# Self attention of a Perceiver-like block: the mix of values of each tile in two halves, with the output product of the tile before it between them

## The chip, the core and the metric

The kernel runs on one core of one Trainium2 chip. The metric is device time in microseconds (us) of one execution, lower is better. A core has a matrix engine (TensorE, PE in the profile; its weight loads are listed apart as PEld), a vector engine (VectorE, DVE), a scalar engine (ScalarE, ACT), GpSimd (POOL) and SyncE (SP), which here only issues DMAs. The engines run their own instruction streams and meet at semaphores.

## What is computed

The reference is a stack of six residual blocks over x of 64 batches, 32 tokens, 256 features:

```python
x = x + _L0_xattn_ref(ctx_1024, _layernorm(x), ...)
x = x + _L0_attn_ref(_layernorm(x), ...)      # stage "sa0" of the kernel
x = x + _L0_ffn_ref(_layernorm(x), ...)       # mixture of 64 experts
x = x + _L1_xattn_ref(_layernorm(x), ctx_1024, ...)
x = x + _L1_attn_ref(_layernorm(x), ...)      # stage "sa1"
x = x + _L1_ffn_ref(_layernorm(x), ...)
```

The change touches the two self attentions. The first, shortened:

```python
q = rms_norm(proj(Wq), qn_w)          # 16 heads of 16 features
k = rms_norm(proj(Wk), kn_w)
v = proj(Wv)
scores = jnp.einsum('bhnd,bhmd->bhnm', q, k) * scale
attn = jax.nn.softmax(scores, axis=-1)
out = jnp.einsum('bhnm,bhmd->bhnd', attn, v)
return out.transpose(0, 2, 1, 3).reshape(B, N, D) @ Wo.T
```

The second (sa1) has latent queries and keys of 32 features for each head, a rotary turn, a causal mask and biases, and is otherwise alike.

## The kernel before

Both attentions are one function, `self_attention`, called once as stage sa0 and once as stage sa1. It works on NT = 16 tiles of 128 tokens (4 batches of 32 tokens each). It is a software pipeline written by hand: every engine runs the same loop over steps n from -6 to 16, and in step n it works on different tiles at different distances: a stage of the work that is called with n + 4 is four tiles ahead of the tile whose output is being finished. The order of the calls in `step` of each engine is the order of its instructions; nothing is scheduled by a planner.

In step n TensorE does, in this order: the scores of tile n + 1 (`scores`, 64 matmuls of 32x32, each of them two instructions in the trace since the data is float32); the transposes of the queries and keys of tile n + 2 (`queries_keys_T`, 8); the transpose of the normalised rows of tile n + 5 (`rows_T`, 2); the output product of tile n - 1 (`output`, 2 matmuls of 128x256, 4 in the trace); the mix of the values of tile n by its probabilities (`mix`, 64 matmuls of 32x32, 128 in the trace, after which ScalarE copies the result to yT); in sa1 one product for the latent queries (`latent_T`); and the projections of tile n + 4 (`values`, `project`). `mix` writes columns 128 to 191 of the PSUM banks 4 to 7, and `scores` writes columns 0 to 127 of the same banks. That is why `mix(n)` waits for `s.shift` of tile n + 1: VectorE has to be done with reading the scores of tile n + 1 before TensorE writes to these banks.

VectorE does in step n: `shifted(n + 1)`, which is a maximum over the scores (L2163) and their subtraction (L2167) and ends with `s.shift`; `add(n - 1)`, which waits for `s.o_ps` of the output product and adds it to the residual (L2186), with the statistics of the next norm behind it; `softmax(n + 1)` (L2172 to L2180), which ends with pT, the transposed probabilities that `mix(n + 1)` reads; then rows (L163), `queries_keys` (L2158 or L2150) and `key_sums` or `cosines` (L2132 or L2142) of tiles further ahead.

ScalarE takes the exponential (L2331) once shifted is done, and copies PSUM to SBUF (mix_T at L2337 writes yT).

Of the kernel before, what the change touches and what calls it, by code (L numbers as in the profile page):

```python
# [25 lines left out]
B, S, D = 64, 32, 256  # L26
NT = B * S // P
BT = P // S
FC = D // P
# [2036 lines left out]
def self_attention(kit, stage, weights, norm, ahead, extra, after):  # L2066


    nc = kit.nc
# [4 lines left out]
    VB = 5  # L2074
# [3 lines left out]
    with kit.stage() as st:  # L2078
        m = kit.buffers(
            st, xl=([P, 2, D], F32), xlT=([P, 2, FC, P], F32), qk=([P, 2, 2 * H, S], F32), v=([P, VB, H, S], F32), qT=([P, 2, HC, P], F32), kT=([P, 2, HC, P], F32),  # L2080
            score=([P, H, S], F32), top=([P, H], F32), prob=([P, H, S], F32), mass=([P, H], F32), rmass=([P, H], F32), pT=([P, 2, H, S], F32), yT=([P, FC, P], F32))
# [4 lines left out]
        else:  # L2086
            r = kit.buffers(st, raw=([P, 2, 512], F32), sq=([P, 512], F32), ss=([P, 2 * H], F32), rss=([P, 2, 2 * H], F32), gain=([P, 1], F32))
            w = wm.w
        s = kit.sems(stage, "zero one masked gain qb xl xlT_ps xlT qk_ps v_ps sq raw v ss scaled rss lat cosed turned qk qT_ps kT_ps qrT qrT_ps qT kT s_ps "
                     "top shift p mass rmass prob pT y_ps yT o_ps biased x_add passed")  # L2090
# [6 lines left out]
        mixed = kit.all[:, 4:8, P:P + FC * S].rearrange("p b (f q) -> p b f q", f=FC)  # L2097

        def place(h):

            return h % BT * HC + h // BT

        def past(engine, sem, value):

            if value > 0:
                engine.wait_ge(sem, value)
# [6 lines left out]
        with nc.Block(no_gpsimd_drain=True) as block:  # L2113
# [249 lines left out]
            def _(pe):  # L2363
                def rows_T(n):
                    pe.wait_ge(s.xl, n + 1)
                    past(pe, s.xlT, n)
                    for f in range(FC):
                        mm = nc.tensor.transpose(kit.psum(0)[:, f * P:(f + 1) * P], m.xl[:, n % 2, f * P:(f + 1) * P], kit.ident[:])
                    mm.then_inc(s.xlT_ps, 1)
# [8 lines left out]
                def values(n):  # L2378
                    pe.wait_ge(s.xlT, n + 1)

                    past(pe, s.x_add, n - 4)
                    past(pe, s.v, n * 2)
                    product(kit.psum(1)[:, D:2 * D], n, slice(QK, QK + D), rotary).then_inc(s.v_ps, 1)

                def project(n):
                    pe.wait_ge(s.xlT, n + 1)

                    past(pe, s.qT, n - 1)
                    past(pe, s.kT, n - 1)
                    if rotary:  # L2390
                        past(pe, s.lat, n * 2)
                        past(pe, s.cosed, n * 2)
                    else:
                        past(pe, s.raw, n)
                    for i in range(QK // 512):
                        product(kit.psum(2 + i), n, slice(i * 512, (i + 1) * 512), rotary).then_inc(s.qk_ps, 1)

                def queries_keys_T(n, more):
                    pe.wait_ge(s.qk, n + 1)

                    if more:
                        if rotary:
                            pe.wait_ge(s.lat, n * 2 + 4)
                            pe.wait_ge(s.cosed, n * 2 + 4)
                        else:
                            pe.wait_ge(s.raw, n + 2)
                    for i, done in enumerate((s.qT_ps, s.kT_ps)):
                        for c in range(HC):
                            mm = nc.tensor.transpose(kit.psum(2 + i)[:, c * P:(c + 1) * P], m.qk[:, n % 2, (i * HC + c) * BT:(i * HC + c + 1) * BT, :].rearrange("p h l -> p (h l)"), kit.ident[:])
                        mm.then_inc(done, 1)  # L2410

                def latent_T(n):
                    pe.wait_ge(s.qrT, n + 1)
                    nc.tensor.matmul(kit.psum(2), wm.wqk[:], r.qrT[:], start=True, stop=True).then_inc(s.qrT_ps, 1)

                def scores(n):
                    if n == 0 and extra is not None:

                        pe.wait_ge(extra.w, 1)
                    pe.wait_ge(s.qT, n + 1)  # L2420
                    pe.wait_ge(s.kT, n + 1)

                    past(pe, s.yT, n - 1)
                    if rotary:
                        if n == 0:
                            pe.wait_ge(s.masked, 1)
                        for a in range(BT):
                            nc.tensor.matmul(kit.all[:, 4 + a, 0:P], kit.ident16[:], r.causal[:].rearrange("p c k -> p (c k)"), start=True, stop=False, skip_group_check=True)
                    for c in range(HC):
                        for b in range(BT):  # L2430
                            for a in range(BT):
                                rows, tokens = slice(a * S, (a + 1) * S), slice(b * S, (b + 1) * S)
                                mm = nc.tensor.matmul(score[tokens, a, c, :], m.qT[rows, n % 2, c, tokens], m.kT[rows, n % 2, c, tokens],
                                                      start=not rotary, stop=True, skip_group_check=True)
                    mm.then_inc(s.s_ps, 1)

                def mix(n, more):
                    pe.wait_ge(s.pT, n + 1)

                    if more:  # L2440
                        pe.wait_ge(s.shift, n + 2)
                    for f in range(FC):
                        for i in range(2):
                            for a in range(BT):
                                for b in range(BT):
                                    rows, part, h = slice(b * S, (b + 1) * S), slice(a * S, (a + 1) * S), f * 2 * BT + 2 * a + i
                                    mm = nc.tensor.matmul(mixed[part, b, f, :], m.v[rows, n % VB, h, :], m.pT[rows, n % 2, place(h), :],
                                                          start=(i == 0), stop=(i == 1), skip_group_check=True)
                    mm.then_inc(s.y_ps, 1)

                def output(n):
                    pe.wait_ge(s.yT, n + 1)

                    pe.wait_ge(s.v, min(n + 5, NT) * 2)
                    past(pe, s.x_add, n)
                    for f in range(FC):
                        mm = nc.tensor.matmul(kit.psum(1)[:, 0:D], m.yT[:, f, :], wm.wo[:, f, :], start=(f == 0), stop=(f == FC - 1))
                    mm.then_inc(s.o_ps, 1)

                def step(n, has):  # L2460
                    if has(1):
                        scores(n + 1)
                    if has(2):
                        queries_keys_T(n + 2, has(3))
                    if has(5):
                        rows_T(n + 5)
                    if has(-1):
                        output(n - 1)
                    if has(0):
                        mix(n, has(1))  # L2470
                    if rotary and has(2):
                        latent_T(n + 2)
                    if has(4):
                        values(n + 4)
                        project(n + 4)

                    if extra is not None and n == -4:
                        extra.first_product(pe)
                    if extra is not None and n == -3:
                        extra.second_product(pe)  # L2480

                if rotary:
                    pe.wait_ge(s.one, 1)
                pe.wait_ge(weights.loaded, weights.count)
                steps(step)


# [787 lines left out]
```

## Time and profile before

| what | value |
|---|---|
| time before, median of 3 runs | 2607.31 us (2605.54 to 2607.59) |
| the profiled execution, its own time | 2623.12 us |
| span in the profile | 2620.9 us |
| TensorE busy | 2451.8 us, 94% of the span |
| VectorE / ScalarE / GpSimd busy | 1690.8 / 1282.5 / 1474.9 us |
| stage sa0, steps with a mix | about 1279 to 1420 us of the span |
| stage sa1, steps with a mix | about 2431 to 2594 us of the span |

The profiled execution took 0.6% more than the median of the runs that were only timed. Rows of the timeline give start and duration in us, the engine, the line of the kernel, the operation, the tile written and the tiles read, and in brackets for how long the engine had been idle and what ended this. "issue" means that no semaphore event explains the idle time. Busy time of TensorE is that of pipelined instructions, so a busy TensorE is not one at its peak.

### The profile page before, as it was taken

The page shows a single profiled execution, that of the slowest core. Times are in us where ns is not written, and L with a number is a line of the kernel's source. Part 1 is how long each engine was busy: PE and PEld are TensorE (multiplying, and loading weights), DVE is VectorE, ACT ScalarE, POOL GpSimd, SP SyncE. Part 2 cuts the span into 40 slices and gives each one's busy share as a digit, 9 for nine tenths or more (in the row PEclk, how much of TensorE's full clock was granted, in tenths as well). Part 3 has the DMA queues.
Part 4 walks back from the last instruction along what each step waited for, and adds up shares of the span by engine and source line. Part 5 has one row for each costly group of instructions (what it writes and reads, how often), then busy time and mean ns, then how long its engine had stood idle before and what let it go on. Part 6 is the DMA issues. An engine that isn't in the chain of part 4 may idle for free. (4 is left out here: it accounts for less than half of the span.)

```text
span 2620.9 us, 64331 instructions
## 1 busy us (share of the span) xinstructions
PE 2451.8 (94%) x24513; PEld 1907.7 (73%) x24513; DVE 1690.8 (65%) x3969; ACT 1282.5 (49%) x2972; POOL 1474.9 (56%) x1669
## 2 busy tenths in 40 slices
PE   6898999999999999998797999599999999998997
PEld 3456788887887878786565588578888888886665
DVE  5677868686868677774475844466656655654665
ACT  3565656565656565654342333244454445543343
POOL 6897767575767675764672254664456445322233
PEclk9999999999999999998897999799999999999999
DMA  4232212121111121210002469542234323210001
GB/s 165 101 149 84 61 35 50 31 49 37 43 40 45 35 50 32 48 30 10 30 5 96 139 195 304 167 116 75 69 95 103 74 68 95 71 45 15 3 4 35
DMA packets 224819, 190.03 MB, mean 73 GB/s; under 512 B 89218, under 2 KB 212675, under 8 KB 224515
## 3 DMA queue, kind: packets, MB, share of 16 engines
q1 hardware_dynamic: 208994, 153.92, 20.0%
q0 software_dynamic: 9216, 27.28, 4.3%
q10 hardware_dynamic: 6304, 4.72, 0.6%
q8 instruction: 198, 3.24, 0.5%
q14 instruction: 107, 0.87, 0.1%
HBM read 151.53 MB, written 34.31 MB: 71 GB/s over the span
## 5 line engine op out<-in xcount | busy, mean ns | idle before, releaser
L295 POOL TENSOR_TENSOR rk<-ss,neg_half 128x32 f32<-128x32 f32 x64 | 348.7, 5449 | 245.3 <-DVE ss L277 245.3
L1779 PE MATMUL banks<-rowsT,qk 128*128 128x257 f32 x1024 | 245.5, 383 | 5.8 <-issue 5.8
L328 ACT ACTIVATE ksq<-kT 128x512 f32<-128x512 f32 x256 | 161.1, 630 | 159.5 <-DVE kT L271 159.5
L1779 PEld LDWEIGHTS banks<-rowsT,qk 128*128 128x128 f32 x1024 | 191.1, 192 | 33.1 <-issue 6.1
L271 DVE COPY kT<-banks 128x512 f32<-128x512 f32 x256 | 176.8, 691 | 59.1 <-PE banks L382 54.9
L382 PE MATMUL banks<-x_hi,wk_hi 128*128 128x256 f32 x1024 | 213.0, 289 | 1.1 <-DVE kT L271 1.0
L382 PE MATMUL banks<-x_hi,wk_lo 128*128 128x256 f32 x1024 | 206.3, 284 | 0.0
L382 PE MATMUL banks<-x_lo,wk_hi 128*128 128x256 f32 x1024 | 205.1, 281 | 0.3 <-DVE x_lo L263 0.3
L1230 ACT ACTIVATE score<-score,ntop 128x289 f32<-128x289 f32 x256 | 135.4, 530 | 115.5 <-DVE ntop L1110 115.4
L1617 POOL CAST r_hi<-diff 128x512 fp32r<-128x512 f32 x64 | 43.0, 672 | 252.7 <-PE banks L1805 249.8
L1588 POOL DMA_INDIRECT parts<-scratch_expert,address x128 | 131.6, 1028 | 90.1 <-DVE residual L1482 45.9
L382 PEld LDWEIGHTS banks<-x_hi,wk_hi 128*128 128x128 f32 x1024 | 159.0, 189 | 3.9 <-issue 3.2
L382 PEld LDWEIGHTS banks<-x_lo,wk_hi 128*128 128x128 f32 x1024 | 159.7, 190 | 0.6 <-DVE x_lo L263 0.5
L382 PEld LDWEIGHTS banks<-x_hi,wk_lo 128*128 128x128 f32 x1024 | 158.0, 188 | 0.0
L1680 ACT ACTIVATE prob<-banks,ntop 128x257 f32<-128x257 f32 x256 | 120.2, 479 | 73.1 <-DVE ntop L1500 68.6
L1500 DVE TENSOR_REDUCE ntop<-banks 128x2 f32<-128x514 f32 x128 | 88.5, 692 | 103.4 <-PE banks L1779 99.7
L1107 DVE CUSTOM_DVE_ANT_0 score<-banks,rkb 128x289 f32<-128x289 f32 x256 | 107.8, 457 | 63.2 <-PE banks L1297 55.0
L1688 ACT CAST p_hi<-banks 128x512 fp32r<-128x512 f32 x128 | 68.7, 589 | 161.4 <-PE banks L1788 153.3
L1244 ACT COPY mix<-banks 128x512 f32<-128x512 f32 x128 | 75.1, 587 | 112.7 <-PE banks L1323 112.7
L1805 PE MATMUL banks<-p_hi,r_hi 128*128 128x512 f32 x256 | 112.9, 441 | 3.3 <-ACT p_hi L1688 3.3
L1513 DVE TENSOR_TENSOR p_lo<-banks,p_hi 128x512 fp32r<-128x512 f32 x128 | 82.4, 685 | 50.3 <-ACT p_hi L1688 50.3
L1323 PE MATMUL banks<-p_hi,r_hi 128*128 128x512 f32 x256 | 114.5, 447 | 0.0
(362 smaller groups left out, 6560.4 us busy)
## 6 DMA issues: line engine op xcount, KB each, us to landing
rowsT<-in_ctxT SPq DMA_DIRECT2D x64, 257.0 KB
wgu<-in_expert_gu SPq DMA_DIRECT2D x64, 256.0 KB
rows<-in_ctx SPq DMA_DIRECT2D x64, 256.0 KB
raw<-in_ctx SPq DMA_DIRECT2D x61, 256.0 KB
scratch_qT<-qT SPq DMA_DIRECT2D x16, 512.0 KB, 2.6
scratch_kT<-kT SPq DMA_DIRECT2D x16, 512.0 KB, 3.0
q<-scratch_qT SPq DMA_DIRECT2D x64, 128.0 KB
kT<-scratch_kT SPq DMA_DIRECT2D x64, 128.0 KB
```

The lines of the kernel that those rows point to most:

```text
L271: nc.vector.tensor_copy(m.kT[:, k, 2 * i:2 * i + 2, 0:ROWS], banks[i % 2].rearrange("p (a r) -> p a r", a=2)).then_inc(s.kT, 1)
L295: nc.gpsimd.tensor_tensor(m.rk[:], m.ss[:], kit.neg_half[:, 0:KF * H], ALU.pow).then_inc(s.rk, 1)
L328: nc.scalar.activation(m.ksq[:, 2 * i:2 * i + 2, :], m.kT[:, k, 2 * i:2 * i + 2, 0:ROWS], ACT.Square).then_inc(s.ksq, 1)
L382: mm = nc.tensor.matmul(banks[i % 2][:, a * ROWS:(a + 1) * ROWS], w[:, f, pr * P:(pr + 1) * P], x[:, k, f, :], start=(at == 0), stop=(at = ...
L1107: nc.vector.tensor_tensor_reduce(m.score[:, c, :], score[c][:, 0:NK], m.rkb[:, c, :], 1.0, -3.0e38, ALU.mult, ALU.max, m.top[:, c:c + 1]). ...
L1230: nc.scalar.activation(m.score[:, c, :], m.score[:, c, :], ACT.Exp, bias=m.ntop[:, c:c + 1], accum_out=m.mass[:, c:c + 1]).then_inc(s.p, 1)
L1323: mm = nc.tensor.matmul(mix_bank[f], lhsT, rhs, start=(at == 0), stop=(at == len(terms) - 1))
L1500: nc.vector.tensor_reduce(m.ntop[:, n % 2, h * HALF:(h + 1) * HALF], score[h][:, :, 0:CTX], AX.X, ALU.max, negate=True).then_inc(s.ntop, 1)
L1588: nc.gpsimd.indirect_dma_start(m.parts[:, t % 2, c, :], None, d.expert_rows, bass.IndirectOffsetOnAxis(kept.address[:, t, c:c + 1], 0)).th ...
L1680: nc.scalar.activation(m.prob[:, k, c, :], score[h][:, c - h * HALF, 0:CTX], ACT.Exp, bias=m.ntop[:, k, c:c + 1], accum_out=m.mass[:, k, c ...
L1779: mm = nc.tensor.matmul(score[h][:, c - h * HALF, 0:CTX], m.qk[:, f, j, c * BT:(c + 1) * BT, :].rearrange("p h q -> p (h q)"), m.rowsT[:, ...
L1805: mm = nc.tensor.matmul(kit.bank[3][:, f, :], lhsT, rhs, start=(at == 0), stop=(at == len(terms) - 1))
```

## The change

`mix` takes a half, f = 0 or 1 (8 of the 16 heads), and is called twice in each step, with `output(n - 1)` between the calls. The waits of `mix` all stand ahead of the first half, among them a new one for yT of the tile before (ScalarE has read the mix that the new one overwrites; before, it was implied by the wait in `output`). The semaphore y_ps is raised after the second half as before. Number and shapes of the matmuls are the same.

```diff
-                def mix(n, more):
-                    pe.wait_ge(s.pT, n + 1)
-
-                    if more:
-                        pe.wait_ge(s.shift, n + 2)
-                    for f in range(FC):
-                        for i in range(2):
...
+                def mix(n, f, more):
+
+                    if f == 0:
+                        pe.wait_ge(s.pT, n + 1)
+
+                        past(pe, s.yT, n)
+                        if more:
+                            pe.wait_ge(s.shift, n + 2)
+                    for i in range(2):
+                        for a in range(BT):
+                            for b in range(BT):
...
+                    if f == FC - 1:
+                        mm.then_inc(s.y_ps, 1)
...
+                    if has(0):
+                        mix(n, 0, has(1))
+
                     if has(-1):
                         output(n - 1)
                     if has(0):
-                        mix(n, has(1))
+                        mix(n, 1, has(1))
```

The order of TensorE's instructions in one full step of sa0, as a difference of the two programs (qk: queries and keys to be transposed; xl: normalised rows; yT with flat: the output product; pT with v: the mix; each row is a run of like instructions with its count):

```order
 L2409 MATMUL banks<-ident,qk 128x128 x8
 L2368 MATMUL banks<-ident,xl 128x128 x2
-L2457 MATMUL banks<-flat,yT 128x256 x2
-L2447 MATMUL banks<-pT,v 32x32 x64
+L2449 MATMUL banks<-pT,v 32x32 x32
+L2460 MATMUL banks<-flat,yT 128x256 x2
+L2449 MATMUL banks<-pT,v 32x32 x32
 L2375 MATMUL banks<-flat,xlT 128x256 x2
```

The output product has moved behind the first 32 matmuls of the mix, and with them behind all that the mix waits for.

The last instructions of TensorE in sa1, before the change (wo with yT is the output product, causal and kT with qT are the scores; the last three tiles end here):

```order
L2433 MATMUL banks<-kT,qT 32x32 x64
L2457 MATMUL banks<-wo,yT 128x256 x2
L2447 MATMUL banks<-pT,v 32x32 x64
L2457 MATMUL banks<-wo,yT 128x256 x2
L2447 MATMUL banks<-pT,v 32x32 x64
L2457 MATMUL banks<-wo,yT 128x256 x2
```

And the same place after it:

```order
L2433 MATMUL banks<-kT,qT 32x32 x64
L2449 MATMUL banks<-pT,v 32x32 x32
L2460 MATMUL banks<-wo,yT 128x256 x2
L2449 MATMUL banks<-pT,v 32x32 x64
L2460 MATMUL banks<-wo,yT 128x256 x2
L2449 MATMUL banks<-pT,v 32x32 x32
L2460 MATMUL banks<-wo,yT 128x256 x2
```

The output product of tile 14 now stands behind the first half of the mix of tile 15, whose probabilities VectorE makes last; the run of 64 is the second half of tile 14 and the first of tile 15.

## Rows read from the trace of the kernel before

**Rows 1.** Busy time by stretch; last: granted clock, DMA share, GB/s.

```profile
1280.00:1420.00 140.00, 113.88 (x4101) 82.68 (x4088) 89.50 (x183) 51.30 (x116) 80.18 (x41) 0.88 0.02 4
2450.00:2590.00 140.00, 131.96 (x3733) 87.45 (x3731) 91.55 (x171) 53.64 (x113) 43.01 (x48) 0.97 0.02 4
```

**Rows 2.** Timeline of all engines, one step of sa0: start, duration.

```profile
1343.96 0.68 DVE L2163 TENSOR_REDUCE top<-banks 128x16 f32<-128x512 f32 x1
1344.68 0.69 DVE L2167 TENSOR_TENSOR score<-banks,top 128x512 f32<-128x512 f32 x1
1344.96 0.73 PEld L2457 LDWEIGHTS banks<-flat,yT 128*128 128x128 f32 x4
1345.07 1.03 PE L2457 MATMUL banks<-flat,yT 128*128 128x256 f32 x4
1346.02 0.91 PEld L2447 LDWEIGHTS banks<-pT,v 32*32 32x32 f32 x97 [0.33 <-issue]
1346.13 0.42 DVE L2186 TENSOR_TENSOR residual<-residual,banks 128x256 f32<-128x256 f32 x1 [0.76 <-PE banks L2457]
...
1347.41 1.16 PEld L2375 LDWEIGHTS banks<-flat,xlT 128*128 128x128 f32 x6
...
1350.19 0.82 PEld L2433 LDWEIGHTS banks<-kT,qT 32*32 32x32 f32 x87 [0.76 <-issue]
...
1350.93 0.69 DVE L2132 TENSOR_REDUCE ss<-sq 128x32 f32<-128x512 f32 x1
```

**Rows 3.** Timeline of VectorE, the maximum over the scores, four of 12 steps.

```profile
1285.09 0.68 DVE L2163 TENSOR_REDUCE top<-banks 128x16 f32<-128x512 f32 x1
...
1368.02 0.68 DVE L2163 TENSOR_REDUCE top<-banks 128x16 f32<-128x512 f32 x1
...
1375.76 0.68 DVE L2163 TENSOR_REDUCE top<-banks 128x16 f32<-128x512 f32 x1
...
1386.23 0.69 DVE L2163 TENSOR_REDUCE top<-banks 128x16 f32<-128x512 f32 x1 [0.47 <-PE banks L2433]
```

**Rows 4.** Timeline of TensorE, a step of sa0 with idle time by "issue".

```profile
1334.20 1.10 PE L2457 MATMUL banks<-flat,yT 128*128 128x256 f32 x4 [1.45 <-issue]
...
1338.01 0.25 PE L2447 MATMUL banks<-pT,v 32*32 32x32 f32 x5 [1.54 <-issue]
1338.19 4.50 PE L2375 MATMUL banks<-flat,xlT 128*128 128x256 f32 x8
```

**Rows 5.** The page's DMA queues: packets, MB, share.

```profile
q8 instruction: 198, 3.24, 0.5%
```

**Rows 6.** Timeline, step 0 of sa0, which has no output product yet.

```profile
1278.61 0.69 DVE L2167 TENSOR_TENSOR score<-banks,top 128x512 f32<-128x512 f32 x1
...
1279.42 0.24 PEld L2447 LDWEIGHTS banks<-pT,v 32*32 32x32 f32 x23 [0.49 <-issue]
```

**Rows 7.** Timeline, one step of sa1.

```profile
2511.89 0.69 DVE L2167 TENSOR_TENSOR score<-banks,top 128x512 f32<-128x512 f32 x1
...
2512.26 0.73 PEld L2457 LDWEIGHTS banks<-wo,yT 128*128 128x128 f32 x4
...
2513.33 1.27 PEld L2447 LDWEIGHTS banks<-pT,v 32*32 32x32 f32 x128 [0.33 <-issue]
...
2514.65 0.30 PEld L2414 LDWEIGHTS banks<-qrT,wqk 128*128 128x128 f32 x2
```

**Rows 8.** Timeline of TensorE, a step of sa1 with idle time by "issue".

```profile
2446.07 0.26 PE L2447 MATMUL banks<-pT,v 32*32 32x32 f32 x7 [1.74 <-issue]
```

**Rows 9.** Timeline, the last steps of sa1.

```profile
2585.90 0.69 DVE L2167 TENSOR_TENSOR score<-banks,top 128x512 f32<-128x512 f32 x1
2586.51 0.41 DVE L2186 TENSOR_TENSOR residual<-residual,banks 128x256 f32<-128x256 f32 x1
...
2587.85 0.86 PE L2447 MATMUL banks<-pT,v 32*32 32x32 f32 x78 [0.49 <-issue]
...
2590.43 0.60 PE L2447 MATMUL banks<-pT,v 32*32 32x32 f32 x46
```

More of the change, by code:

```diff
@@ L2435, in scores @@
                     mm.then_inc(s.s_ps, 1)
-                def mix(n, more):
-                    pe.wait_ge(s.pT, n + 1)
-                    if more:
-                        pe.wait_ge(s.shift, n + 2)
-                    for f in range(FC):
-                        for i in range(2):
[L2444 to L2449, printed above, removed]
+                def mix(n, f, more):
[7 more added lines that the diff above has]
+                            for b in range(BT):
+                                rows, part, h = slice(b * S, (b + 1) * S), slice(a * S, (a + 1) * S), f * 2 * BT + 2 * a + i
+                                mm = nc.tensor.matmul(mixed[part, b, f, :], m.v[rows, n % VB, h, :], m.pT[rows, n % 2, place(h), :],
+                                                      start=(i == 0), stop=(i == 1), skip_group_check=True)
+                    if f == FC - 1:
+                        mm.then_inc(s.y_ps, 1)
                 def output(n):
```

## The prediction

> **What bounds the kernel now.** I read the busy time by stretch first, then the timeline of one step in each stage, then TensorE's idle time. In sa1 TensorE is busy for 131.96 of 140 us: it is the bound there. In sa0 it is busy for 113.88 of 140, and its granted clock is 0.88 on the mean [rows 1]. So sa0 wants a closer look.
>
> In a quiet step of sa0 TensorE and VectorE are balanced. Step to step (maximum to maximum) it takes 1375.76 - 1368.02 = 7.74 us, and seven of the 11 steps between the first and the last row of that group take 7.6 to 8.4, 54.9 us in all. The other four take 10.5 to 12.6, together 46.25, of the 101.14 us from first to last [rows 3]. What makes them long is idle time of TensorE put down to "issue" in the middle of runs of identical matmuls that wait for nothing: 1.45 us ahead of the output product, and then 1.54 inside the mix [rows 4]. The two ends of these gaps lie 1338.01 - 1334.20 = 3.81 us apart, with 127 matmuls and as many weight loads between. I read this as instruction supply: about 256 instructions arrive as one block, and the next takes 3.8 us from the moment the last was begun. The queue of kind "instruction" moved 3.24 MB in 198 packets, 16 KB each [rows 5]. The Trainium skill (Advanced Engine Details and Errata, section ISA Cache) says that a line of the instruction cache is 16 KB, 256 instructions. By that rule, the trace agrees in both numbers. The supply allows two blocks in 7.6 us; a step needs about 2.2, so every fourth step or so has a third block and is long.
>
> **The change part by part.** No matmul is added or removed. What moves: the output product (4 instructions of TensorE) goes behind the wait for shift and behind 64 of the mix's 128 instructions. Behind it on TensorE stand the second half, the projections and the next scores; the one who waits for it is VectorE's add, and behind the add on VectorE stand the norm's statistics, the softmax of tile n + 1, rows, queries and keys, key sums, and the next shifted.
>
> *Step of sa1, TensorE's side.* The subtraction ends at 2511.89 + 0.69 = 2512.58 [rows 7]. How long TensorE takes to start after it is seen in step 0, which has no output product: 1278.61 + 0.69 = 1279.30, first load of the mix at 1279.42, so 0.12 us [rows 6]. The first half starts then at 2512.70, where the output product's first load stood at 2512.26: 0.44 us lost. It was the output product that filled this gap. The rest keeps its length: output to mix 1.07 (2513.33 - 2512.26), mix to the next product 1.32 (2514.65 - 2513.33) [rows 7], to be cut in two halves of 0.65. The array is switched between 128x128 and 32x32 two times more in each step. The switch from 128 to 32 shows 0.33 us without a weight load [rows 2, 7], but this is inside the 1.07; the one from 32 to 128 shows no gap (mix loads end, and the projection's begin at 1347.41 with none noted [rows 2]). I take 0.05 for the extra pair; the bounds are 0 and 2 x 0.33. The Trainium skill (TensorEngine Tiling (Array Packing), Key Properties) says that a change of the tiling mode drains TensorE, which speaks against cutting the mix in two. The trace agrees only in part: loads of the mix start at 1346.02, 0.08 before the output's last matmul ends [rows 2].
>
> Per full step of sa1: 0.44 + 0.05 = 0.5 us. VectorE has room there (91.55 of 140 us busy [rows 1]). There are 12 such steps. In two of them TensorE stands still inside the mix, 1.74 us in the one shown [rows 8]; the block that is waited for was begun ahead of the output product and comes at the same time as now, so these lose nothing. 10 x 0.5 = **5.0 us**.
>
> *Step of sa0, VectorE's side.* Call the end of the subtraction S = 1345.37. Now the add starts at 1346.13, S + 0.76. After the change: 0.12 to the first half, 0.65 + 0.05 for it, and from the output's first load to its end 1.14 (1346.10 - 1344.96), 0.03 to the add: S + 2.0. From the add to the next maximum VectorE works without a break: the key sums start 4.80 after the add (1350.93 - 1346.13), and the maximum can follow 0.62 behind (VectorE's short operations follow each other so): 5.42. From the maximum to S it is 1.41 [rows 2]. Sum: 5.42 + 1.41 + 2.0 = 8.83 us per step. TensorE's side of the same loop: from the add, 0.6 to the projections, 2.78 for them (1350.19 - 1347.41), 1.35 for the scores: 4.72 [rows 2], less than 5.42. So VectorE becomes the bound of a quiet step, with 0.7 us of slack on TensorE. Seven quiet steps: 7 x 8.83 - 54.9 = +6.9 us.
>
> In the four long steps instruction supply is late anyway, and the longer step gives it time. For the step of [rows 4], with T the start of a block 1.2 us ahead of the scores' end: the first half waits for T + 3.85, the output ends at T + 5.7, the second half meets the next block's end at T + 7.65, the next maximum falls at T + 11.85, after one at T + 1.9: 9.95 us where 10.8 would stand without the slow clock. I take -0.6 for each of the four, -2.4 together (bounds: -1.0 and +1.0 each). Sum for the middle of sa0: **+4.5 us**.
>
> *The ends.* In the last steps nothing is left to hide behind, and tile 15's softmax stands behind the add of tile 13 on VectorE. In sa1 this add starts at 2586.51. After the change: S = 2586.59, first half from 2586.71, held inside until the block at 2587.85, done at 2588.0, output product done at 2589.15, add at 2589.2, 2.7 us later. The probabilities are 2.7 later, the mix of tile 15 starts at 2593.1 in place of 2590.43, and the output product of tile 14 (1.1 us) now stands inside it, less the 0.7 of a block that has come by then: +3.0 us [rows 9]. The same in sa0, where the output products run at half clock but the mix of tile 15 waits for one already: I take +1.7 us (between 0.8 and 3). Together **+4.7 us**.
>
> Sum: 5.0 + 4.5 + 4.7 = +14.2 us, against the profiled execution's 2623.12 us: 2637.3. The runs' median lies 0.6% below that, which changes 14.2 by less than 0.1: 2607.3 + 14.2 = 2621.5 us.
>
> **The rivals.**
> 1. *As above* (0.61): 2621.5 us, and between 2614 and 2630 by its bounds.
> 2. *Supply sets sa0's pace whatever the order* (0.15). For it: 2.2 blocks by 3.81 is 8.4 us per step, near the 9.2 on the mean now (101.14 / 11). Then sa0 loses nothing in the middle or at its end, and 5.0 + 3.0 = 8 stay: 2615 us. Against it: the quiet steps run at 7.74.
> 3. *The clock falls more often* (0.08). The projections of [rows 4] took 4.50 us where the quiet step has 2.85: 1.65 more, after TensorE stood still twice in 5 us; this is the lower level, 1.2 GHz in place of 2.4. The change puts an idle of 0.4 to 1.1 us in each step. If five more steps of sa0 fell, 5 x 1.65 = 8 us more: 2630 us.
> 4. *The switches cost in full* (0.04): 2 x 0.33 in each of 28 steps is 18.5 us in place of 1.4, added to 14.2: 2638 us. This is what the drain rule of the Trainium skill's page on array packing (Key Properties) would mean at its worst. Against it stands the overlap of 0.08 us in [rows 2].
> 5. *Supply is relieved* (0.06), the other side. A run of 128 matmuls and 128 loads uses a block in 1.3 us, far faster than 3.8; with an output product and a wait inside, the run takes 2.8. If this freed the four long steps, they would go from 46.25 to 4 x 8.83 = 35.3: 11 us back; in sa1 the two stalled steps 1.74 each and the slow clock behind them, another 6. Then 14.2 + 2.4 - 17 = -0.4, and with other gaps inside the mixes gone, about -7: 2600 us. It decides from 14 us of relief on. Against it: the block is late by its count of instructions per step, which the change leaves as it is.
> 6. *The wait is passed already* (0.06): if shift were done when TensorE comes to the first half, only the add moves. It would need TensorE 0.44 us later than in [rows 7]. About 0 to 4 us: 2609 us.
>
> **How the numbers follow.** A measurement of this kernel can tell about 0.2%, 5.2 us, from no change: faster is below 2602.1, slower above 2612.5. Case 5 gives most of faster (0.05); same is the rest of 5 and most of 6 and the low edge of 2 (0.08); slower 0.87. The range 2611 to 2634 leaves out cases 4, 5, part of 6 and the upper part of 3.
>
> **What would show it.** Right: the first half's load 0.12 us after the subtraction ends, in nearly every step; VectorE's idle ahead of L2186 grown from 0.76 to 2.0 us in quiet steps of sa0, and these at 8.8 us; sa1 steps 0.5 us longer; the last add of sa1 some 3 us further behind the last scores. Wrong: quiet steps of sa0 still at 7.7, fewer or shorter "issue" gaps inside the mix, a mean clock in 1280 to 1420 other than about 0.88, or the extra time outside the two stages.

## The result and the profile after

The changed kernel takes 2627.96 us (median of 3 runs, 2623.99 to 2629.17) against 2607.31 us before: the ratio is 1.0063, 95% interval 1.0048 to 1.0077. It is slower, by 16.4 us at this ratio; 14.2 were forecast. A second comparison, in other rounds, gave 1.0064 (1.0048 to 1.0080).

The profiled execution of after has a span of only 4.8 us more than that of before:

```profile
span 2625.7 us, 64318 instructions
```

The rest is chance between executions in stages that the change does not touch: from the last output product of sa0 to the first maximum over the scores of sa1 it is 1001.5 us before (1417.99 to 2419.48) and 992.0 after (1421.33 to 2413.32); over the 14 traces of this document it ranges from 992.0 to 1014.0. So I compare stretches inside the two stages, by the starts of L2163 on VectorE and of the output products on TensorE.

VectorE in the middle of sa0 after the change, the rows that answer to [rows 2, 3]:

```profile
1359.38 0.68 DVE L2163 TENSOR_REDUCE top<-banks 128x16 f32<-128x512 f32 x1
1362.77 0.42 DVE L2186 TENSOR_TENSOR residual<-residual,banks 128x256 f32<-128x256 f32 x1 [1.99 <-PE banks L2460]
1368.04 0.68 DVE L2163 TENSOR_REDUCE top<-banks 128x16 f32<-128x512 f32 x1
```

VectorE now sits idle for 1.99 us ahead of each add, where it was 0.76, and the quiet step takes 1368.04 - 1359.38 = 8.66 us in place of 7.74. In the same step TensorE (loads and matmuls in order):

```profile
1359.85 0.38 PE L2368 MATMUL banks<-ident,xl 128*128 128x128 f32 x2
1360.09 0.69 DVE L2167 TENSOR_TENSOR score<-banks,top 128x512 f32<-128x512 f32 x1
1360.90 0.66 PEld L2449 LDWEIGHTS banks<-pT,v 32*32 32x32 f32 x64 [0.91 <-issue]
1360.93 0.74 PE L2449 MATMUL banks<-pT,v 32*32 32x32 f32 x64 [0.70 <-DVE score L2167]
1361.60 0.73 PEld L2460 LDWEIGHTS banks<-flat,yT 128*128 128x128 f32 x4
...
1362.66 0.64 PEld L2449 LDWEIGHTS banks<-pT,v 32*32 32x32 f32 x64 [0.33 <-issue]
...
1363.34 1.16 PEld L2375 LDWEIGHTS banks<-flat,xlT 128*128 128x128 f32 x6
```

The subtraction ends at 1360.78, the first half's load comes 0.12 us later, and TensorE has by then stood idle for 0.70 us. From the first half's load to the projections' it is 1363.34 - 1360.90 = 2.44 us. In sa1 the same place, which answers to [rows 7]:

```profile
2530.36 0.69 DVE L2167 TENSOR_TENSOR score<-banks,top 128x512 f32<-128x512 f32 x1
2530.51 0.25 PEld L2368 LDWEIGHTS banks<-ident,xl 128*128 128x128 f32 x2
...
2531.16 0.66 PEld L2449 LDWEIGHTS banks<-pT,v 32*32 32x32 f32 x64 [0.40 <-issue]
...
2531.87 0.73 PEld L2460 LDWEIGHTS banks<-wo,yT 128*128 128x128 f32 x4
...
2532.93 0.64 PEld L2449 LDWEIGHTS banks<-pT,v 32*32 32x32 f32 x64 [0.33 <-issue]
...
2533.61 0.30 PEld L2414 LDWEIGHTS banks<-qrT,wqk 128*128 128x128 f32 x2
```

TensorE's loads pause for 0.40 us where those of the output product followed the transposes at once. A quiet step of sa1 is 11.43 to 11.45 us (10.84 before). The end of sa1 on TensorE, with the one add on VectorE that the last mix hangs on; it answers to [rows 9]:

```profile
2587.19 0.27 PE L2449 MATMUL banks<-pT,v 32*32 32x32 f32 x10 [1.04 <-issue]
2587.39 1.75 PE L2460 MATMUL banks<-wo,yT 128*128 128x256 f32 x4
...
2593.10 0.88 PE L2449 MATMUL banks<-pT,v 32*32 32x32 f32 x64 [3.15 <-DVE pT L2180]
2593.91 2.08 PE L2460 MATMUL banks<-wo,yT 128*128 128x256 f32 x4
...
2597.27 2.07 PE L2460 MATMUL banks<-wo,yT 128*128 128x256 f32 x4 [0.47 <-ACT yT L2337]
```

```profile
2584.66 0.69 DVE L2167 TENSOR_TENSOR score<-banks,top 128x512 f32<-128x512 f32 x1
2589.18 0.42 DVE L2186 TENSOR_TENSOR residual<-residual,banks 128x256 f32<-128x256 f32 x1 [3.83 <-PE banks L2460]
```

The add of tile 13 starts 3.8 us after the subtraction has ended; before, it did not wait for it at all. TensorE waits 3.15 us for the probabilities of tile 15, and its last output products take 2.08 us where those of before took 1.13:

```profile
2589.18 1.13 PE L2457 MATMUL banks<-wo,yT 128*128 128x256 f32 x4 [0.47 <-ACT yT L2337]
...
2593.08 1.13 PE L2457 MATMUL banks<-wo,yT 128*128 128x256 f32 x4 [0.47 <-ACT yT L2337]
```

After the change they run at the lower level of the clock, 1.2 GHz: the granted clock is 0.50 on the mean from 2593.1 to 2599.4, and was 1.00 from 2585.2 to 2594.3 before.

By stretch, in us (16 maxima in each stage; "middle" is from the 3rd to the 14th of them, 11 steps; "end" is from the 14th to the start of the last output product):

| trace | sa0 quiet step | sa0 middle | sa0 end | sa1 quiet step | sa1 middle | sa1 end |
|---|---|---|---|---|---|---|
| before | 7.74 | 101.1 | 31.8 | 10.84 | 128.5 | 23.7 |
| before, second trace | 7.45 | 99.7 | 30.8 | 10.84 | 130.3 | 23.9 |
| after | 8.66 | 105.6 | 33.3 | 11.43 | 130.9 | 31.6 |
| after, second trace | 8.68 | 103.9 | 32.9 | 11.44 | 130.7 | 30.1 |

Quiet steps repeat to 0.02 us, except those of before in sa0; the middle stretches hold some steps of 10 to 14 us that do not.

### The profile page after: what moved, and what is told of

Same layout as the page of the kernel before. It is cut to its first block and busy times, and to the rows that moved or that the text cites. A ratio compares the mean times of both kernels' runs of the same rounds, so it can differ in the third digit from the quotient of the medians.

```text
span 2625.7 us, 64318 instructions
## 1 busy us (share of the span) xinstructions
PE 2448.2 (93%) x24498; PEld 1905.0 (73%) x24513; DVE 1691.0 (64%) x3969; ACT 1282.6 (49%) x2972; POOL 1475.5 (56%) x1669
## 5 line engine op out<-in xcount | busy, mean ns | idle before, releaser
L1680 ACT ACTIVATE prob<-banks,ntop 128x257 f32<-128x257 f32 x256 | 120.2, 479 | 70.2 <-DVE ntop L1500 70.2
```

The source lines that it names most:

```text
L1680: nc.scalar.activation(m.prob[:, k, c, :], score[h][:, c - h * HALF, 0:CTX], ACT.Exp, bias=m.ntop[:, k, c:c + 1], accum_out=m.mass[:, k, c ...
```

## The experiments

Ratios are to the kernel before, timed in the same rounds. Where a stage is not touched by an experiment, its stretches are further traces of that order.

**The wait alone.** The mix is whole and behind the output product; the output product waits for shift too.

```diff
                 def output(n):
                     pe.wait_ge(s.yT, n + 1)
+                    if n + 3 <= NT:
+                        pe.wait_ge(s.shift, n + 3)
```

> The mix is whole and stands behind the output product as before; the output product alone is made to wait for shift too. No switch of the array is added. If the cost comes from the wait standing ahead of the output product: sa1's quiet steps 0.4 to 0.5 us longer, quiet steps of sa0 at about 8.2 us (the add 1.3 us after the subtraction in place of 0.76, TensorE 0.45 us later), together 8 to 12 us more than before. If it comes from cutting the mix in two: no more than 2 us.

Ratio 1.0002 (0.9986 to 1.0017): no difference, against 8 to 12 us expected. The trace (sa0, VectorE, with TensorE's loads of the mix and of the projections):

```profile
1321.13 0.68 DVE L2163 TENSOR_REDUCE top<-banks 128x16 f32<-128x512 f32 x1
...
1323.67 1.18 PEld L2447 LDWEIGHTS banks<-pT,v 32*32 32x32 f32 x128 [0.33 <-issue]
1323.78 0.42 DVE L2186 TENSOR_TENSOR residual<-residual,banks 128x256 f32<-128x256 f32 x1 [1.24 <-PE banks L2459]
...
1324.88 1.16 PEld L2375 LDWEIGHTS banks<-flat,xlT 128*128 128x128 f32 x6
...
1329.06 0.68 DVE L2163 TENSOR_REDUCE top<-banks 128x16 f32<-128x512 f32 x1
```

The quiet step of sa0 is 7.93 us, not 8.2: from the add to the next maximum VectorE needs 1329.06 - 1323.78 = 5.28 us, less than my 5.42. sa1's quiet step is 11.22, 0.38 over 10.84. By these sizes I would still expect 5 us, and the interval reaches to 4.5. The middle of sa0 came out at 98.7 and its end at 29.5, lower than in both traces of before (a third one with the order of before in this stretch, that of the last experiment, has 98.7 too); sa1 has 128.7 and 24.9. TensorE's idle by "issue" in sa0 is 18.0 us here, against 23.5 and 23.9 before: where the quiet steps grew, TensorE stood still less elsewhere. That this is what pays for the wait is read from one trace, not shown. So the wait costs a quiet step what was read for it, and the kernel as a whole nothing that can be measured.

**The cut alone.** Output product first, as before; the transposes of the next rows between the halves.

```diff
-                    if has(5):
-                        rows_T(n + 5)
                     if has(-1):
                         output(n - 1)
                     if has(0):
-                        mix(n, has(1))
+                        mix(n, 0, has(1))
+                    if has(5):
+                        rows_T(n + 5)
+                    if has(0):
+                        mix(n, 1, has(1))
```

> The mix is cut in two, but the output product stands ahead of it as before, and the transposes of the next rows (L2368) stand between the halves: two more switches of the array in each step, and no wait ahead of the output product. If the wait is the cost: within 2 us of before (0.05 us for 28 steps is 1.4). If the switches cost 0.33 us each: 9 to 18 us more.

Ratio 1.0020 (1.0005 to 1.0035), 5 us: between the two sizes expected, within 2 us and 9 to 18. Loads of TensorE in a step of sa0:

```profile
1315.21 0.64 PEld L2449 LDWEIGHTS banks<-pT,v 32*32 32x32 f32 x64 [0.33 <-issue]
...
1315.90 0.20 PEld L2368 LDWEIGHTS banks<-ident,xl 128*128 128x128 f32 x2
...
1316.27 0.64 PEld L2449 LDWEIGHTS banks<-pT,v 32*32 32x32 f32 x64 [0.17 <-issue]
...
1316.95 1.16 PEld L2375 LDWEIGHTS banks<-flat,xlT 128*128 128x128 f32 x6
```

From the mix to the projections 1.74 us; the whole mix took 1.21 in the experiment above (1323.67 to 1324.88) and the transposes take 0.22 elsewhere, so the two extra switches cost 0.31 here, and sa1's quiet step shows the same (11.14, 0.30 over 10.84). In sa0 it is hidden (7.70). Between the halves of the change itself it is less: 2.44 against 1.07 + 1.21 = 2.28, so 0.16 in sa0, and 11.43 - 11.22 = 0.21 in sa1. I had taken 0.05. The Trainium skill (TensorEngine Tiling (Array Packing), Key Properties) says that a change of the tiling mode drains TensorE; here the trace agrees that a pair of changes costs something, and puts it at 0.16 to 0.31 us.

**One stage alone.** sa1 keeps its order.

```diff
-                    if has(0):
+                    if has(0) and not rotary:
                         mix(n, 0, has(1))
                     if has(-1):
                         output(n - 1)
+                    if has(0) and rotary:
+                        mix(n, 0, has(1))
                     if has(0):
                         mix(n, 1, has(1))
```

> The change in sa0 alone; sa1 keeps the order of before. By the two traces sa0 gives 6 us and sa1 10 us of the change's cost: 6 us more than before here. If the 0.63% came from outside the two stages or from chance between executions, the two stages' shares would not show in this way.

Ratio 1.0039 (1.0020 to 1.0057). sa0: quiet 8.68, middle 103.9, end 33.2, as in after; sa1: 10.84, 127.9, 22.2, as before. The costs belong to their stages. The ratio says 10 us for sa0 where the traces say 6; its interval, 5 to 15 us, holds both.

**The ends alone.** The order of before in the last three steps.

```diff
+                    last = n >= NT - 3
-                    if has(0):
+                    if has(0) and not last:
                         mix(n, 0, has(1))
                     if has(-1):
                         output(n - 1)
+                    if has(0) and last:
+                        mix(n, 0, has(1))
```

> The change in all steps but the last three (n = 13, 14, 15), which have the order of before. If the ends of the stages cost what the traces show (2 us in sa0, 7.9 us in sa1), this is 7 to 10 us faster than the changed kernel and 7 to 9 us slower than before; the adds of tiles 13 and 14 come early again. If the end of sa1 cost 3 us only, as predicted, and the rest is the clock's chance, it is 4 to 5 us faster than the changed kernel.

Ratio 1.0035 (1.0023 to 1.0047), 9 us where the whole change has 16. The ends are 30.8 us in sa0 and 24.8 in sa1, within about 1 us of before, and the last output product of sa1 takes 1.13 us again:

```profile
2606.83 1.13 PE L2460 MATMUL banks<-wo,yT 128*128 128x256 f32 x4 [0.47 <-ACT yT L2337]
```

So the six changed steps at the two ends carry nearly half of the cost, 7 us, with each of the two ratios good to some 3 us.

**The add behind the softmax**, with the change (first) and without it (second):

```diff
                     if has(1):
                         shifted(n + 1)
-                    if has(-1):
-                        add(n - 1)
                     if has(1):
                         softmax(n + 1)
+                    if has(-1):
+                        add(n - 1)
```

> The changed kernel, but on VectorE the add of tile n - 1 stands behind the softmax of tile n + 1. If sa0's cost is VectorE waiting for an output product that comes 2.0 us after the subtraction: its idle ahead of the add falls to about 0, that ahead of the softmax is 0.7 us (it waits for the exponential), a quiet step of sa0 falls from 8.67 to 8.0 (TensorE is the bound then), and the last mix no longer waits 2.7 to 3.2 us for its probabilities: 8 to 14 us faster than the changed kernel, all in sa0 and in the two ends; sa1's quiet step stays at 11.43. If the cost sits in TensorE's own order (wait and switches), sa0 stays as it is.

> The kernel before, with VectorE's add behind the softmax and nothing else. Its idle ahead of the add is 0.76 us and the one ahead of the softmax would be 0.69, so quiet steps stay at 7.7 and 10.84 us; at the two ends the last softmax comes 0.5 to 1 us earlier. Within 3 us of before. It shows how much of what e5 gains is owed to the change.

Ratios 1.0046 (1.0033 to 1.0060) and 1.0065 (1.0052 to 1.0079). The first is some 4 us faster than the changed kernel, where 8 to 14 were expected; the second is 17 us slower than the kernel before, where 3 at most were. Both expectations failed in the middle of sa0: the quiet step is 9.05 us in both. In the second, sa1's quiet step is 11.50 too, not 10.84. The trace of the first, around the projections:

```profile
1356.42 0.38 DVE L2186 TENSOR_TENSOR residual<-residual,banks 128x256 f32<-128x256 f32 x1
1356.87 1.16 PEld L2375 LDWEIGHTS banks<-flat,xlT 128*128 128x128 f32 x6 [1.00 <-issue]
...
1360.38 0.69 DVE L2132 TENSOR_REDUCE ss<-sq 128x32 f32<-128x512 f32 x1 [1.55 <-ACT sq L2289]
1360.99 0.68 DVE L2163 TENSOR_REDUCE top<-banks 128x16 f32<-128x512 f32 x1
```

VectorE's idle ahead of the add is gone, as expected. But `values` waits for this add (`past(pe, s.x_add, n - 4)`; the values and the output product share a PSUM bank), and its load stands still for 1.00 us until 0.07 us after the add's end. What VectorE gave up TensorE waits for, and VectorE gets it back as 1.55 us of idle ahead of the key sums. In sa1 of the second kernel the load of the values also starts 0.07 us after the add's end, behind 0.58 us without a load. I had not looked for who waits for the add on TensorE. The ends behave as expected in the first: 31.2 and 25.2 us, in place of 33.3 and 31.6, since no projections are left there. So the add standing ahead of the last softmaxes is what made the ends long. The lower clock by itself is not: it is here as well in the last part of sa1 (granted clock 0.59 from 2591.2 to 2601.8),

```profile
2596.31 2.08 PE L2460 MATMUL banks<-wo,yT 128*128 128x256 f32 x4
```

and the end of sa1 is still only 1.4 us longer than before.

**The output product behind the whole mix.**

```diff
                     if has(0):
                         mix(n, 0, has(1))
+                        mix(n, 1, has(1))
                     if has(-1):
                         output(n - 1)
-                    if has(0):
-                        mix(n, 1, has(1))
```

> The output product behind the whole mix: no switch more than before, the wait ahead of the first half as in the change, and the add 0.6 us later still. If VectorE's wait sets sa0's pace: quiet steps of sa0 at 8.67 + 0.6 = 9.3 us, sa1's at 11.43 - 0.2 = 11.2 (one pair of switches less). If the switches were the cost in sa0, its quiet steps fall below 8.67.

Ratio 1.0184 (1.0168 to 1.0200). Quiet steps of sa0 9.23 us (expected 9.3), with one row of VectorE for the reason:

```profile
1376.43 0.42 DVE L2186 TENSOR_TENSOR residual<-residual,banks 128x256 f32<-128x256 f32 x1 [2.55 <-PE banks L2460]
```

With fewer switches than the change it is slower in sa0, so the switches are not the cost there. Four traces now stand on one line, 5.28 us from the add to the next maximum, 1.41 to the end of the subtraction, and VectorE's idle: 0.76 gives 7.45 (the second trace of before has it), 1.24 gives 7.93, 1.99 gives 8.68, 2.55 gives 9.24; measured 7.45, 7.93, 8.66, 9.23. This is the sum of the parts of VectorE's own loop; what it shows is that VectorE has no other idle time in these steps. In sa1 the quiet step is 11.4 to 11.6, not 11.2; `values` waits for the late add here too, in part. The quiet steps are the smaller part of the 48 us that the ratio stands for: the middle of sa0 takes 120.2 us, with three steps of 14.0 to 14.6 us at a granted clock of 0.65 to 0.76, its end 37.0, and sa1 135.6 and 32.8.

**Half of the mix's matmuls left out**, in the kernel before; the output lacks the second head of each pair.

```diff
-                        for i in range(2):
+                        for i in range(1):
...
-                                                          start=(i == 0), stop=(i == 1), skip_group_check=True)
+                                                          start=True, stop=True, skip_group_check=True)
```

> The kernel before without the half of the mix's matmuls that adds the second head of each pair: 64 matmuls and 64 loads less of TensorE in each step, about 440 instructions in place of 566. If the idle time inside the runs of small matmuls is the supply of blocks of 256 instructions, 3.8 us each: 1.7 blocks in 7.6 us, so the long steps of 10 to 12.6 us in the middle of sa0 go, and its 11 steps take 83 to 88 us in place of 101. If the idle time has another cause (the clock, a queue of another engine), two to four long steps stay.

The long steps are gone. The 3rd and the 14th maximum:

```profile
1283.68 0.69 DVE L2163 TENSOR_REDUCE top<-banks 128x16 f32<-128x512 f32 x1 [0.17 <-PE banks L2433]
...
1364.26 0.68 DVE L2163 TENSOR_REDUCE top<-banks 128x16 f32<-128x512 f32 x1
```

11 steps in 80.6 us (83 to 88 expected), none over 7.8. 0.65 us less of matmuls in each step explains 7 of the 20 us saved there; the others were the long steps. TensorE's idle by "issue" in sa0 falls from 23.5 us to 2.8. Ratio 0.9834 (0.9817 to 0.9852), 43 us in all. The idle time inside the small matmuls depends on how many instructions a step has, as supply in blocks says.

**The projections between the output product and the mix**, sa0, in the kernel before; ScalarE's `inner(n + 4)` goes ahead of `mix_T(n)`.

```diff
                     if has(-1):
                         output(n - 1)
+                    if not rotary and has(4):
+                        project(n + 4)
                     if has(0):
                         mix(n, has(1))
...
                         values(n + 4)
-                        project(n + 4)
+                        if rotary:
+                            project(n + 4)
```

> The kernel before with one change in sa0 alone: the projection of tile n + 4 (2.8 us with the values; 1.7 without) stands between the output product and the mix, so that the two runs of 256 small instructions, scores and mix, lie 1.7 us further apart; ScalarE takes the projection ahead of the mix. If the supply of instruction blocks (3.8 us each) sets the long steps: quiet steps stay near 7.7 (TensorE's work is the same; a wait of up to 0.4 us for ScalarE's copy of the keys may be added), and the four long ones lose 0.5 to 2 us each: 2 to 8 us faster than before. If the supply is bound by its rate alone, the time stays, as a step still needs 2.2 blocks.

Ratio 1.0058 (1.0042 to 1.0073), 15 us slower instead of 2 to 8 us faster; the middle of sa0 takes 111.7 us and its shortest steps 8.3. TensorE:

```profile
1308.90 0.54 PE L2436 MATMUL banks<-kT,qT 32*32 32x32 f32 x39 [1.95 <-issue]
...
1312.29 1.96 PE L2378 MATMUL banks<-flat,xlT 128*128 128x512 f32 x4 [0.74 <-ACT kT L2318]
```

Two things: the projection waits 0.74 us for ScalarE's copy of the keys (0.4 at most was expected), and the mix now lies close to the next scores, so the idle of 1.5 to 2 us stands inside the scores. In all TensorE's idle by "issue" in sa0 is 28.4 us, against 23.5 and 23.9 in the traces of before. Moving work between the runs of small instructions moves the gap; it does not remove it.

**Both kernels once more**, for second traces and a second ratio.

> The kernel before, once more, for a second trace. If the two slow stretches of the projections in the middle of sa0 (steps of 12.5 us) are the rule, they are here again, and the 11 steps take about 101 us; if they are chance of that one execution, the 11 steps take 96 to 99 us, and the change's cost in the middle of sa0 is 7 to 9 us instead of 4.4. Quiet steps 7.74 and 10.84 us in either case.

> The changed kernel once more, for a second trace and a second ratio: 1.0063 again, quiet steps of 8.67 and 11.43 us, 11 steps in the middle of sa0 at 103 to 106 us, and the last three steps of sa1 with output products at half clock, 12 to 13 us from the last maximum to the last output product.

The second trace of before has no step of 12.5 us in sa0 (its five long ones are 9.8 to 11.3, four at a granted clock of 1.00 and one at 0.84) and 99.7 us for the middle, between the two values expected; three of its quiet steps take 7.40 to 7.46, where 7.74 was expected in either case. That of after has 103.9 for the middle. The difference is 4.2 us, as between the first traces (4.4). The second ratio is 1.0064. TensorE's idle by "issue" in sa0 fell from 23.5 and 23.9 us to 16.2 in both traces of after. From the last maximum of sa1 to the last output product it is 11.9 us in the second trace of after (12 to 13 expected; 13.3 in the first), and the mix of tile 15 waits as in the first:

```profile
2602.30 0.89 PE L2449 MATMUL banks<-pT,v 32*32 32x32 f32 x64 [3.19 <-DVE pT L2180]
```

The output product of tile 13 takes 1.13 us there, those of tiles 14 and 15 take 2.08.

**The last softmax ahead of the add, at the ends only**, in the kernel before: the exchange of the two calls as above, under `n >= NT - 4`. It was the candidate for a version faster than both.

> The kernel before; on VectorE the add of tile n - 1 stands behind the softmax of tile n + 1 in the last steps only (n = 12 to 15), where TensorE has no projections left that would wait for the add. If the end of a stage is set by the softmax of the last tile standing behind an add, the stretch from the 14th maximum to the last output product falls from about 31 to 29.5 us in sa0 and from 23.8 to 22.8 in sa1, and nothing else moves: 2 to 3 us faster than before, about 0.1%. If the ends are set by instruction supply: no change.

Ratio 1.0006 (0.9993 to 1.0019): not faster. The ends are 30.5 us in sa0 and 22.6 in sa1; in the other traces with the order of before at the ends they are 30.7 to 31.8 and 22.2 to 24.8. If it gains, it is less than the spread. No version here that computes the whole result beats the kernel before.

## Why the prediction was right, point by point

- **What bounds each stage.** Right. sa1's steps grow by what TensorE loses, sa0's by what VectorE waits; the four traces on one line show the second.
- **Supply of instructions in blocks of about 256, 3.8 us each.** The experiment with half of the mix bears it out, and so does the shift of the gaps with the projections between. That it is a fetch is shown by the DMA packets in the traces: in the four traces of the two kernels TensorE is idle by "issue" for more than 0.6 us 62 times in the two stages, and each of these times ends 1.21 to 1.59 us after a 16 KB packet of the queue of kind "instruction" has landed; of moments drawn at random in these stages, 7 to 9% would. For the two gaps of [rows 4], which end at 1334.20 and 1338.01, the packets landed at 1332.61 and 1336.54. In both stages such packets begin no closer than 3.3 us to each other, so the period of 3.8 us is near the shortest seen and not a constant. The Trainium skill (Advanced Engine Details and Errata, section ISA Cache) names 256 instructions as the size of a cache line, which this count agrees with.
- **sa1, quiet step.** Forecast 0.49 us, measured 0.59. The wait was mis-sized at 0.44 and is 0.38; the switches were taken as 0.05 and are 0.21. "10 x 0.5 = 5.0" is to be held against 130.9 and 130.7 after, and 128.5, 130.3, 127.9, 124.4 and 122.0 in the five traces with sa1's order unchanged: +4.2 on the mean, with 8 us of spread.
- **sa0, middle.** Forecast 8.83 us for a quiet step, measured 8.66 (the stretch from the add to the next maximum is 5.28, not 5.42), and +4.5 for the middle; measured +4.4 and +4.2. Both parts of the term hold in the first traces: the seven steps that were quiet before grew from 54.9 to 62.5 us (+7.6, forecast +6.9), the four that were long shrank from 46.3 to 43.1 (-3.2, forecast -2.4). The clock helped with the second: the steps of 12.6 and 12.5 us of before had a granted clock of 0.73 and 0.86 on the mean.
- **The ends.** The term that was mis-sized. Forecast +1.7 in sa0: measured about +2 (33.3, 32.9, 33.2 against 31.8, 30.8). Forecast +3.0 in sa1: measured 31.6 and 30.1 against 23.7 and 23.9, +7.9 and +6.2. The mechanism is as told; the term "the mix of tile 15 starts at 2593.1 in place of 2590.43, and the output product of tile 14 (1.1 us) now stands inside it" counts too little of it, in two places.
  First, it begins at the last subtraction. The two steps ahead of it, from the 14th to the 16th maximum, take 18.2 us in both traces where they took 15.8 and 15.9: +2.4 and +2.3, of which the forecast has 0.5 per step at most. With the add behind the softmax they take 15.2.
  Second, the time from the last maximum to the last output product grew by 5.4 and 3.9 us. In the second trace of after the mix of tile 15 starts 6.32 us after the subtraction has ended, and 6.51 were forecast; in the first it is 7.75, behind 1.04 us of idle by "issue" and a slow output product of tile 13 (1.75 us). From there to the last output product both traces take 4.2 us where the forecast has 3.05, since this part runs at the lower clock: the output product of tile 14 takes 2.08 us, not 1.1. The step before the last maximum is at the lower clock for longer too (granted clock 0.65 and 0.66 on the mean, 0.80 and 0.79 before); from its transposes to its scores it takes 7.96 us against 6.59, and with 0.2 of this for the switches I estimate 1.2 us as the clock's. It was rival 3, the clock, in a place where I had not put it: by this estimate 2.3 us of the +6.2 and 2.9 of the +7.9, and most of the rest goes with the late adds, as the experiment with the add behind the softmax shows.
  That the waits are what lowers the clock is read from these traces and was not tried by itself; with the order of before in the last three steps the granted clock is 1.00 (2599.0 to 2608.0) and these products take 1.13 again.
- **The sum.** 14.2 forecast, 16.4 by the ratio. The stretches of the first two traces give 4.4 + 1.5 + 2.5 + 7.9 = 16.3 us, those of the second two 4.2 + 2.2 + 0.4 + 6.2 = 13.0; means over more traces give 18. Single traces cannot do better than some us. That the sum comes so close is in part luck: the end of sa1 was taken 3 to 5 us too low, and in the same two pairs of traces the middle of sa1 came out 2.5 and 4.6 us under its term.
- **The rivals.** Supply that sets the pace whatever the order: no, the middle of sa0 is 4 us longer. Supply relieved: in part true, 7.5 us of TensorE's idle went in sa0, but VectorE was the bound there by then; what came of it is the 3.2 us that the long steps lost in the first traces, no more. Switches in full: 0.16 to 0.31 per pair, not 0.66. The wait passed already: no, it is seen in every step.
- **My theory was too simple in one place.** I put the cost on the wait. The wait alone gives no measurable loss, the cut alone 5 us, and together with the output product behind 64 matmuls it is 16. In sa0 and at the ends, what costs is how late the output product ends for VectorE: 1.24 us after the subtraction is still nearly free, 1.99 is not, and with 2.55 the kernel loses 48 us, slower clock and ends included. In the middle of sa1, where TensorE is the bound, it is the 0.38 us of the wait and the 0.21 of the switches in each step.

## What to carry to other kernels

In this kernel a product that filled the time until another engine was done cost nothing where it stood; behind the wait it cost its place twice, once on the engine that now idles and once on the engine that waits for its result. Before moving such a product, write down the loop of the engine that waits (its work plus its idle) and compare it with the loop of the mover: the larger one is the step. And look at the last tiles by themselves: nothing else covers a delay there, each late add holds up the softmax behind it, and TensorE came to the lower clock there (a granted clock of 0.62 on the mean from the last maximum of sa1 on, and 1.00 in the kernel before).

## What was not expected of the hardware

- In the middle of sa0 a pair of switches between 128x128 and 32x32 costs 0.16 us around a product of four matmuls and 0.31 us around one of two short transposes. Where both were on TensorE's path (sa1), steps grew by 0.21 and 0.30.
- The same program's untouched stages differ by several us from one execution to the next: 1001.5 and 992.0 us between the two attentions in the first traces of before and after, 992.0 to 1014.0 over all 14.
- TensorE stands still for 16 to 24 us of sa0 without waiting for any engine, mostly in the middle of runs of 32x32 matmuls, and goes on 1.2 to 1.6 us after a packet of instructions has landed.
